# Row scaling of two RMS norms moved from VectorE to ScalarE, tile by tile

## The chip, the cores and the metric

The kernel runs on one core of a Trainium2 chip. The metric is the device time of one execution in microseconds (us), lower is better. TensorE is called PE, VectorE DVE, ScalarE ACT and GpSimd POOL, as in the profile; SP issues DMAs. Each engine runs its own instructions strictly in order, and the engines meet only at semaphores.

## The reference, cut to what matters

`x` has 64 batches of 32 rows of 128. It passes through three blocks, each added to x: a cross-attention block, two layers with delta-rule attention (x turned to 32 sequences of 64 steps), and a mixture of experts. The change is in the two layers of the middle block:

```
x = layernorm(x), turned to [32, 64, 128]
for l in range(2):
    h = x * rsqrt(mean(x * x) + 1e-6) * norm1_w[l]      # first norm ("n1")
    x = x + delta_attn(h, ...)                          # projections, chunked solve, Wo
    h = x * rsqrt(mean(x * x) + 1e-6) * norm2_w[l]      # second norm ("n2")
    g, y = split(h @ Wg[l])
    x = x + silu(g) * y @ Wd[l]
x = x * rsqrt(mean(x * x) + 1e-6) * final_norm_w
```

All data are f32. The weights norm1_w and norm2_w are applied later, after the transpose, where they lie one per partition; the norm itself multiplies each row by one number.

## The kernel before, in words

The 2048 rows of the working array R are 16 tiles of 128 rows (partitions) by 128 columns. Four tiles are a group (GT = 4, a [128, 512] piece of R), and two groups a pair: pair A is groups 0 and 1, pair B groups 2 and 3. Each pair goes through the stages of both layers and then through the experts. A string written out by hand (TURNS) says in which order the stages of the two pairs are issued, and every engine walks through the same list STEPS; within a stage it does group 0 of the pair (u = 0) and then group 1 (u = 1). So whatever an engine does for one pair stands in its queue between pieces of the other pair. There is no planner beyond that.

A norm of a group goes over four engines:

- ACT, `squares` (L869): four ACTIVATE Square over [128, 128], each with its row sum into one column of `ss[g]`; the last raises q_ss (n1) or m_ss (n2).
- POOL, `rsqrt` (L995 to L999): add eps (L998), then a power of -0.5 (L999) into `rstd[g]`; raises q_rr or m_rr.
- DVE, `rms_scaled` (L1067): one multiply of [128, 512] by rstd broadcast along the columns, into `yn[g]`; raises q_h or m_h. The stages are at L1319 (n1 of layer 1) and L1398 (n2).
- PE, `transposes` (L506): four transposes of yn into a PSUM bank; then ACT copies the bank to yT with the norm's weight (L892, L950), and the projections (n1) or the gate and up products (n2, L751 and L754) follow.

The n1 of layer 0 is another form (a layernorm and an RMS norm in one, L1308), and the final norm (`fin`, L1409) uses `rms_scaled` as well; neither is touched. yn of pair A is called yn in the profile, yn of pair B act_o. The diff touches six places in the order of STEPS: n2 of layer 0 and n1 of layer 1 for pair A, the same for pair B, then n2 of layer 1 for A and for B. What stands behind them in ACT's queue is, in this order:

- n2 of layer 0, pair A: `ah1` of pair B (evictions of the solve's second half, L926), `wt` of pair B (L933), then A's own copy to yT
- n1 of layer 1, pair A: A's own copy to yT
- n2 of layer 0, pair B: B's own copy to yT
- n1 of layer 1, pair B: B's own copy to yT, then `lout` of pair A (eight copies of the inverted blocks, L920)
- n2 of layer 1, pair A: A's own copy to yT
- n2 of layer 1, pair B: the Silu of an expert step of pair A (L979), then B's own copy to yT

Of the kernel before, what the change touches and what calls it, by code (L numbers as in the profile page):

```python
# [13 lines left out]
D = 128  # L14
NJ = 16
GT = 4
GW = GT * D
NU = 2
# [120 lines left out]
def perceiver(nc, x, ctx_t, ctx_z, ctx_last, rows, cols, w1, w2, wqkvb, wo, wgu, wd, gate_t, gate_bias,  # L139
              we_gate, we_up, we_down, sh_gate, sh_up, sh_down, ident_in, causal_in, spread_in, before_in, out):  # L140
    with ExitStack() as stack:
# [672 lines left out]
        def _(act):  # L814
# [54 lines left out]
            def squares(src, g, done):  # L869
# [3 lines left out]
                                          scale=float(D) ** -0.5, accum_out=ss[g][:, jj:jj + 1])  # L873
                last.then_inc(done, 1)

            act.wait_ge(x_done[1], NU)
            for a in range(NA):
                act.dma_start(*turned(NG - 1, a, 1)).then_inc(x_out, 16)
            act.wait_ge(masks_made, 1)
            for kind, l, pr in STEPS:  # L880
                pi = l * 2 + pr
                for u in range(NU):
# [4 lines left out]
                    if kind == "n1" and l > 0:  # L887
                        act.wait_ge(r2_ready, i - NG + 1)
                        squares(gcols(R, g), g, q_ss)
                    elif kind == "tr":  # L890
                        act.wait_ge(q_tr, i + 1)
                        copy(yT[g][:, :], b0, colv[:, C_N1 + l:C_N1 + l + 1]).then_inc(q_hT, 1)  # L892
                    elif kind in ("pj0", "pj1"):
                        part = int(kind[2])
                        act.wait_ge(q_proj, pi * 4 + part * 2 + u + 1)
                        both = psum[:, bank * 512:(bank + 2) * 512].rearrange("p (j c) -> p j c", j=2)
                        act.activation(qkv[g][:, part * 2:part * 2 + 2, :], both[:, :, 0:3 * D], ACT.Silu)
                        act.activation(th[g][:, part * 2:part * 2 + 2, :], both[:, :, 3 * D:QKVB], ACT.Tanh,
                                       scale=0.5).then_inc(q_silu, 1)
                    elif kind == "sq":  # L900
                        act.wait_ge(q_silu, pi * 4 + 2 + u + 1)
                        act.activation(sq[g].rearrange("p (j c) -> p j c", j=GT), qkv[g][:, :, 0:2 * D],
                                       ACT.Square).then_inc(q_sq, 1)
                    elif kind == "kt0":
                        act.wait_ge(k_tr, 2 * i + 1)
                        for par in range(2):
                            copy(KT[g][par], b0, head_of[par])
                        act.wait_ge(k_tr, 2 * i + 2)
                        copy(QT[g], b1).then_inc(k_bq, 1)
                    elif kind[:4] == "gram":  # L910
                        q = int(kind[4])
                        act.wait_ge(g_mm[u], pi * 4 + q + 1)
                        if q == 0:
                            act.wait_ge(q_vb, i + 1)
                        copy(quarter(GA[g], q), gram_part(bank, 0)).then_inc(g_a[u], 1)
                    elif kind == "ext":
                        act.wait_ge(g_a[u], pi * 4 + 4)
                        copy(chunks_of(pr, u),
                             GA[g].rearrange("p (n c) -> p n c", c=T)[:, :, 0:C16], chunk[0]).then_inc(s_ext0[u], 1)
                    elif kind == "lout":  # L920
                        act.wait_ge(l_inv, pi + 1)
                        lanes = back[pr].rearrange("p (n r) -> p n r", r=C16)[:, u * NB:(u + 1) * NB, :]
                        for j in range(NC):
                            last = copy(TT[g].rearrange("p (n c) -> p n c", c=T)[:, :, j * C16:(j + 1) * C16], lanes, chunk[j])
                        last.then_inc(l_out[u], 1)
                    elif kind[0] == "a":  # L926
                        half = int(kind[2])
                        act.wait_ge(s_a[u], pi * 2 + half + 1)
                        ws, us = ((b0, b1)[half].rearrange("p (t c n) -> p t c n", t=2, c=2)[:, :, c] for c in range(2))
                        copy(WU[g][:, half * 2 * D:(half + 1) * 2 * D].rearrange("p (t n) -> p t n", t=2), ws).then_inc(s_ae[u], 1)  # L930
                        copy(WU[g][:, GW:2 * GW].rearrange("p (b t n) -> p t b n", b=2, t=GT)[:, half * 2:half * 2 + 2],
                             us.rearrange("p t (b n) -> p t b n", b=2)).then_inc(s_ae[u], 1)
                    elif kind == "wt":  # L933
                        act.wait_ge(s_wt[u], pi + 1)
                        copy(WT[g], b0).then_inc(s_wte[u], 1)
                    elif kind == "onorm":
                        act.wait_ge(s_omm[u], pi + 1)
                        own = psum[:, bank * 512:(bank + 2) * 512].rearrange("p (x a e) -> p x a e", a=4, e=DK)[:, :, 0:4:3, :]
                        copy(P1[g].rearrange("p (x a e) -> p x a e", a=2, e=DK), own).then_inc(s_ocp[u], 1)
                        act.wait_ge(s_ocp[u], pi + 1)  # L940
                        act.activation(osq[g], P1[g], ACT.Square, scale=float(DK) ** -0.5).then_inc(s_osq[u], 1)
                    elif kind == "otr":
                        act.wait_ge(o_tr, i + 1)
                        copy(yT[g][:, :], b0, colv[:, C_ON + l:C_ON + l + 1]).then_inc(o_oT, 1)
                    elif kind == "n2":
                        act.wait_ge(r1_ready, i + 1)
                        squares(gcols(R, g), g, m_ss)
                    elif kind == "mtr":
                        act.wait_ge(m_tr, i + 1)
                        copy(yT[g][:, :], b0, colv[:, C_N2 + l:C_N2 + l + 1]).then_inc(m_hT, 1)  # L950
                    elif kind[:2] == "gu":
                        c = int(kind[2])
                        fn = IC[c][1]
                        act.wait_ge(m_gu, 3 * pi * NU + c * NU + u + 1)
                        if c > 0:
                            act.wait_ge(m_a, 3 * pi * NU + (c - 1) * NU + u + 1)
                        act.activation(gate[g][0:fn, :], b0[0:fn, :], ACT.Silu).then_inc(m_silu, 1)
                    elif kind == "fin":
                        act.wait_ge(r2_ready, i + 1)
                        squares(gcols(R, g), g, f_ss)  # L960
                    elif kind == "etr":
                        act.wait_ge(e_tr, g + 1)
                        copy(yT[g][:, :], b0).then_inc(e_hT, 1)
                    elif kind == "elog":
                        act.wait_ge(e_log, g + 1)
                        sg = route[pr][0]
                        act.activation(sg[:, u * GT:(u + 1) * GT, :].rearrange("p j e -> p (j e)"), b1[:, 0:GT * E],
                                       ACT.Sigmoid).then_inc(e_sig, 1)
                    elif kind == "ec":
                        act.wait_ge(e_ctr, g + 1)  # L970
                        copy(cf[g], b0[0:E, :]).then_inc(e_cf, 1)
                    elif kind in ("x0", "x1") and u == int(kind[1]):
                        p, n = l, nth(kind, l)
                        act.wait_ge(x_gate[pr], n + 1)
                        if p < 1 and n > 0:
                            act.wait_ge(x_a[pr], n)
                        elif n > 0:
                            act.wait_ge(x_gu[pr], routed(n))
                        act.activation(act_g[pr], banks[4 * pr + 2 * (n % 2)], ACT.Silu).then_inc(x_silu[pr], 1)  # L979
                    elif kind in ("end0", "end1") and u == int(kind[3]):  # L980
                        act.wait_ge(x_down[pr], (u + 1) * (NPAIR + 1))
                        copy(res[g], banks[4 * pr + 3]).then_inc(e_acc[pr], 1)
# [67 lines left out]
        def _(dve):  # L1050
# [224 lines left out]
            for kind, l, pr in STEPS:  # L1275
# [21 lines left out]
                for u in range(NU):  # L1297
# [10 lines left out]
                    elif kind == "n1" and l == 0:  # L1308
# [4 lines left out]
                        if u == NU - 1:  # L1313
                            for k in range(NU):
# [1 line left out]
                                dve.wait_ge(d_rstd, gk + 1)  # L1316
                                normed(lambda jj: gcols(X, gk)[:, jj * D:(jj + 1) * D],
                                       lambda jj: gcols(R, gk)[:, jj * D:(jj + 1) * D], gk).then_inc(q_r, 1)
                    elif kind == "n1":  # L1319
                        dve.wait_ge(q_rr, i + 1)  # L1320
                        if l == 1:
                            dve.wait_ge(q_r, g + 1)
                        rms_scaled(yn[g], gcols(R, g), g).then_inc(q_h, 1)
                    elif kind == "sq":
                        dve.wait_ge(q_silu, pi * 4 + 2 + u + 1)
                        dve.tensor_scalar(beta[g][:, :, :], th[g][:, :, :], 1.0, None, ALU.add).then_inc(q_beta, 1)
# [68 lines left out]
                    elif kind == "wo":  # L1395
                        dve.wait_ge(o_wo, i + 1)
                        dve.tensor_tensor(gcols(R, g), b1, gcols(R, g), ALU.add).then_inc(r1_ready, 1)
                    elif kind == "n2":  # L1398
                        dve.wait_ge(m_rr, i + 1)
                        rms_scaled(yn[g], gcols(R, g), g).then_inc(m_h, 1)  # L1400
                    elif kind[:2] == "gu":
                        c = int(kind[2])
                        fn = IC[c][1]
# [117 lines left out]
```

## Time and profile before

| | |
|---|---|
| three runs | 691.83, 692.78, 692.90 us; median 692.78 |
| the profiled execution | 694.24 us; its span from first to last instruction 692.4 us |
| mean granted TensorE clock | 0.878 |
| PE busy | 562.5 us (81%), weight loads 366.4 us |
| DVE busy | 442.3 us (64%), 1116 instructions |
| ACT busy | 257.3 us (37%), 576 instructions |
| POOL busy | 78.7 us (11%), 124 instructions |
| DMA | 45.67 MB, 65 GB/s over the span |

How to read it: times are of one profiled execution, counted from its first instruction. Row sums and products follow from busy times, but what an instruction costs the kernel is seen only in the chain of waits and in the timeline, where an idle time before an instruction is shown in brackets with what ended it. A line number can be that of a helper (L816 is every `copy` of ACT, L506 every transpose of a group).

### The profile page before, as it was taken

The page shows a single profiled execution, that of the slowest core. Times are in us where ns is not written, and L with a number is a line of the kernel's source. Part 1 is how long each engine was busy: PE and PEld are TensorE (multiplying, and loading weights), DVE is VectorE, ACT ScalarE, POOL GpSimd, SP SyncE. Part 2 cuts the span into 40 slices and gives each one's busy share as a digit, 9 for nine tenths or more (in the row PEclk, how much of TensorE's full clock was granted, in tenths as well). Part 3 has the DMA queues.
Part 4 walks back from the last instruction along what each step waited for, and adds up shares of the span by engine and source line. Part 5 has one row for each costly group of instructions (what it writes and reads, how often), then busy time and mean ns, then how long its engine had stood idle before and what let it go on. Part 6 is the DMA issues. An engine that isn't in the chain of part 4 may idle for free.

```text
span 692.4 us, 15649 instructions
## 1 busy us (share of the span) xinstructions
PE 562.5 (81%) x6616; PEld 366.4 (53%) x6616; DVE 442.3 (64%) x1116; ACT 257.3 (37%) x576; POOL 78.7 (11%) x124
## 2 busy tenths in 40 slices
PE   5778990767499699977688579879968899999995
PEld 2443570446499576753567558754534344444442
DVE  5785783897867535678647874794476655555553
ACT  2466530564240443552374236225223222222221
POOL 2311230630000011202120011101020000000000
PEclk9998995785556699996899879889998999999998
DMA  8788003000000000000000310003202264343331
GB/s 313 304 310 301 7 12 98 8 1 2 1 3 4 2 2 2 3 2 0 1 2 5 125 71 2 3 7 95 61 1 61 74 150 112 83 128 76 86 88 34
DMA packets 19037, 45.67 MB, mean 66 GB/s; under 512 B 3764, under 2 KB 8500, under 8 KB 18964
## 3 DMA queue, kind: packets, MB, share of 16 engines
q1 hardware_dynamic: 18648, 44.54, 20.8%
q8 instruction: 52, 0.85, 0.5%
q10 hardware_dynamic: 320, 0.13, 0.1%
q14 instruction: 17, 0.14, 0.1%
HBM read 42.30 MB, written 2.36 MB: 65 GB/s over the span
## 4 chain that ended last, share of the span: by engine, by line
PE 58%; DVE 25%; ACT 7%; issue 3%; POOL 2%; SPq 2%; DMA 2%; DVEq 0%; POOLq 0%
PE psum L793 8%; PE psum L798 7%; PE psum L788 7%; PE psum L506 4%; PE psum L635 4%; PE psum L621 3%; PE psum L751 3%; PE psum L754 3%; ACT arena L816 3%; PE psum L663 3%; PE psum L714 2%; PE psum L760 2%; DVE mid L1370 2%; DVE rowv L1368 2%; PE psum L704 2%
## 5 line engine op out<-in xcount | busy, mean ns | idle before, releaser
L979 ACT ACTIVATE arena<-psum 128x512 f32<-128x512 f32 x68 | 40.6, 597 | 126.5 <-PE psum L788 106.3
L1430 DVE TENSOR_TENSOR arena<-psum,arena 128x512 f32<-128x512 f32 x64 | 44.2, 691 | 56.8 <-PE psum L793 55.4
L798 PE MATMUL psum<-arena,wed_sb 128*128 128x512 f32 x128 | 66.2, 599 | 0.0
L621 PE MATMUL psum<-arena 32*64 32x128 f32 x1024 | 42.4, 323 | 17.8 <-DVE XA L1346 10.8
L816 ACT ACTIVATE arena<-psum 128x512 f32<-128x512 f32 (+1 forms) x72 | 34.1, 502 | 56.6 <-PE psum L621 38.5
L1435 DVE TENSOR_TENSOR arena<-arena 128x512 f32<-128x512 f32 x64 | 44.3, 693 | 14.7 <-PE psum L798 12.6
L621 PEld LDWEIGHTS psum<-arena 32*64 32x64 f32 x1024 | 36.4, 163 | 22.6 <-DVE XA L1346 11.8
L793 PE MATMUL psum<-yT,weu_sb 128*128 128x512 f32 x68 | 36.2, 614 | 11.9 <-DVE arena L1430 11.9
L506 PE MATMUL psum<-ident,yn 128*128 128x128 f32 x72 | 15.2, 367 | 36.7 <-DVE yn L1063 22.7
L798 PEld LDWEIGHTS psum<-arena,wed_sb 128*128 128x128 f32 x128 | 24.6, 192 | 31.2 <-issue 21.8
L998 POOL TENSOR_TENSOR ve<-ss,eps_rms 128x4 f32<-128x4 f32 x16 | 4.7, 291 | 292.9 <-ACT yr L872 182.5
L999 POOL TENSOR_TENSOR rstd<-ve,neg_half 128x4 f32<-128x4 f32 x32 | 35.5, 1108 | 2.5
L788 PE MATMUL psum<-yT,weg_sb 128*128 128x512 f32 x68 | 34.8, 593 | 0.0
L788 PE MATMUL psum<-w_sb,weg_sb 128*128 128x512 f32 x68 | 34.7, 592 | 0.0
L793 PE MATMUL psum<-w_sb,weu_sb 128*128 128x512 f32 x68 | 34.7, 592 | 0.0
L506 PEld LDWEIGHTS psum<-ident,yn 128*128 128x128 f32 x72 | 11.5, 190 | 40.1 <-issue 22.2
L506 PE MATMUL psum<-ident,act_o 128*128 128x128 f32 x72 | 13.6, 335 | 20.0 <-DVE act_o L1069 15.0
L793 PEld LDWEIGHTS psum<-yT,weu_sb 128*128 128x128 f32 x68 | 12.7, 193 | 29.9 <-DVE arena L1430 16.0
L816 ACT ACTIVATE yT<-psum,colv 128x512 f32<-128x512 f32 x12 | 8.0, 686 | 44.7 <-PE psum L506 44.7
L506 PEld LDWEIGHTS psum<-ident,act_o 128*128 128x128 f32 x72 | 10.1, 170 | 25.1 <-DVE act_o L1069 16.5
L760 PEld LDWEIGHTS psum<-wd_sb,arena 128*128 128x128 f32 (+1 forms) x192 | 21.9, 191 | 2.2 <-DVE arena L1405 2.2
L635 PE MATMUL psum<-mid,arena 64*64 64x32 f32 x512 | 18.6, 237 | 5.4 <-ACT arena L816 5.4
(294 smaller groups left out, 1172.7 us busy)
## 6 DMA issues: line engine op xcount, KB each, us to landing
arena<-shares SPq DMA_DIRECT2D x64, 256.0 KB, 4.0
arena<-in_ctx_t SPq DMA_DIRECT2D x16, 514.0 KB, 8.3
arena<-in_ctx_z SPq DMA_DIRECT2D x16, 512.0 KB, 9.6
XA<-in_x SPq DMA_DIRECT2D x2, 512.0 KB, 4.9
weg_sb<-in_we_gate SPq DMA_DIRECT2D x2, 512.0 KB, 6.1
weu_sb<-in_we_up SPq DMA_DIRECT2D x2, 512.0 KB, 7.0
wed_sb<-in_we_down SPq DMA_DIRECT2D x2, 512.0 KB, 7.6
x_mid<-XA SPq DMA_DIRECT2D x28, 32.0 KB, 1.9
```

The lines of the kernel that those rows point to most:

```text
L506: last = pe.transpose(bank[:, jj * D:(jj + 1) * D], src[u][:, jj, :], ident[:, :])
L621: last = pe.matmul(banks[bank + hh][s2 * T:(s2 + 1) * T, m * D:(m + 1) * D].rearrange("p (c q) -> p c q", c=2), KT[g][par][rows_, c0:c0 + ...
L635: last = pe.matmul(two_parts(bank[rows_, :], t % 2, h), lhs[rows_, n * T:(n + 1) * T], two_parts(rhs[rows_, :], t, h), start=True, stop=True)
L760: last = pe.matmul(b0[:, jj * D:(jj + 1) * D], hm[g][0:fn, c, jj * D:(jj + 1) * D], wd_sb[0:fn, l, c, :], start=(c == 0), stop=(c == 2))
L788: pe.matmul(banks[4 * pr + 2 * (n % 2)], weg_sb[:, w, :], yT[g][:, :], start=True, stop=True).then_inc(x_gate[pr], 1)
L793: pe.matmul(x1, weu_sb[:, w, :], yT[g][:, :], start=True, stop=True).then_inc(x_up[pr], 1)
L798: pe.matmul(x3, wed_sb[:, (p - 1) % (NPAIR + 1), :], act_a[pr], start=(p == 0), stop=False, skip_group_check=True).then_inc(x_down[pr], 1)
L816: return act.activation(out_, in_, ACT.Copy, scale=scale)
L979: act.activation(act_g[pr], banks[4 * pr + 2 * (n % 2)], ACT.Silu).then_inc(x_silu[pr], 1)
L999: pool.tensor_tensor(rstd[u][:, 0:n], v, neg_half[:, 0:n], ALU.pow).then_inc(done, 1)
L1430: dve.tensor_tensor(act_gu[pr], banks[4 * pr + 1], act_g[pr], ALU.mult).then_inc(x_gu[pr], 1)
L1435: dve.tensor_tensor(act_a[pr], share[pr][k % 2][:, (p % PER) * GW:(p % PER + 1) * GW], act_gu[pr], ALU.mult).then_inc(x_a[pr], 1)
```

## The change

For the touched norms the multiply is taken off DVE. ACT gets a helper `by_row` that waits for rstd of a group and scales its four tiles one by one, each by an ACTIVATE Copy over [128, 128] whose scale is a column of rstd. It is issued for both groups of a pair, behind the squares of the second group. Semaphore values stay as they were; DVE's wait for q_r at n1 goes with its step.

```diff
+            def by_row(g, i, ready, done):
+
+                act.wait_ge(ready, i + 1)
+                for jj in range(GT):
+                    last = copy(yn[g][:, jj, :], gcols(R, g)[:, jj * D:(jj + 1) * D], rstd[g][:, jj:jj + 1])
+                last.then_inc(done, 1)
+
...
                     if kind == "n1" and l > 0:
                         act.wait_ge(r2_ready, i - NG + 1)
                         squares(gcols(R, g), g, q_ss)
+                        if u == NU - 1:
+                            for k in range(NU):
+                                by_row(pr * NU + k, l * NG + pr * NU + k, q_rr, q_h)
...
                     elif kind == "n2":
                         act.wait_ge(r1_ready, i + 1)
                         squares(gcols(R, g), g, m_ss)
+                        if u == NU - 1:
+                            for k in range(NU):
+                                by_row(pr * NU + k, l * NG + pr * NU + k, m_rr, m_h)
...
-                    elif kind == "n1":
-                        dve.wait_ge(q_rr, i + 1)
-                        if l == 1:
-                            dve.wait_ge(q_r, g + 1)
-                        rms_scaled(yn[g], gcols(R, g), g).then_inc(q_h, 1)
...
-                    elif kind == "n2":
-                        dve.wait_ge(m_rr, i + 1)
-                        rms_scaled(yn[g], gcols(R, g), g).then_inc(m_h, 1)
```

## Rows read from the trace of the kernel before

**Rows 1.** The chain that ended last, by engine (share of the span)
```profile
PE 58%; DVE 25%; ACT 7%; issue 3%; POOL 2%; SPq 2%; DMA 2%; DVEq 0%; POOLq 0%
```
**Rows 2.** Instructions of line L1069: duration ns min/median/max, first and last start
```profile
L1069 DVE TENSOR_TENSOR yn<-R,rstd x8: 679/691/693, 248.8 to 431.2; 128x512 f32<-128x512 f32 x8
```
**Rows 3.** Groups of ACT by form: busy us, mean ns, idle before
```profile
L816 ACT ACTIVATE arena<-yr,small 128x512 f32<-128x512 f32 x16 | 10.0, 708 | 3.3 <-DVE yr L1375 3.3
L872 ACT ACTIVATE yr<-R 128x128 f32<-128x128 f32 x32 | 9.4, 296 | 8.0 <-DVE R L1408 4.2 <-DVE R L1397 3.8
L846 ACT ACTIVATE yn<-yr,shift,rstd 128x128 f32<-128x128 f32 x16 | 6.4, 481 | 0.0
```
**Rows 4.** Timeline of ACT: start us, length us, instructions merged
```profile
26.41 3.17 ACT L846 ACTIVATE yn<-yr,shift,rstd 128x128 f32<-128x128 f32 x8
345.10 4.99 ACT L816 ACTIVATE arena<-yr,small 128x512 f32<-128x512 f32 x8
```
**Rows 5.** Chain in order of time, 246 to 252 us: start, length
```profile
246.28 3.85 PE psum L635 x128
250.14 1.14 PE psum L689 x8
```
**Rows 6.** Timeline around n2 of layer 0, pair A
```profile
247.79 1.01 POOL L999 TENSOR_TENSOR rstd<-ve,neg_half 128x4 f32<-128x4 f32 x1
248.51 0.63 ACT L816 ACTIVATE arena<-psum 128x256 f32<-128x256 f32 x2
248.83 0.69 DVE L1069 TENSOR_TENSOR yn<-R,rstd 128x512 f32<-128x512 f32 x1 [1.81 <-POOL rstd L999]
249.04 1.34 POOL L999 TENSOR_TENSOR rstd<-ve,neg_half 128x4 f32<-128x4 f32 x1
250.18 0.66 ACT L816 ACTIVATE arena<-psum 128x256 f32<-128x256 f32 x2 [1.05 <-PE psum L635]
```
**Rows 7.** Timeline around n1 of layer 1, pair A
```profile
272.78 1.01 POOL L999 TENSOR_TENSOR rstd<-ve,neg_half 128x4 f32<-128x4 f32 x1
275.37 1.27 ACT L816 ACTIVATE yT<-psum,colv 128x512 f32<-128x512 f32 x2 [2.94 <-PE psum L506]
```
**Rows 8.** Timeline around n2 of layer 0, pair B
```profile
314.37 1.52 POOL L999 TENSOR_TENSOR rstd<-ve,neg_half 128x4 f32<-128x4 f32 x1
316.40 1.97 PE L506 MATMUL psum<-ident,act_o 128*128 128x128 f32 x8 [7.98 <-DVE act_o L1069]
317.55 0.69 ACT L816 ACTIVATE w_sb<-psum,colv 128x512 f32<-128x512 f32 x1 [4.91 <-PE psum L506]
```
**Rows 9.** Timeline around n1 of layer 1, pair B
```profile
339.10 1.03 POOL L999 TENSOR_TENSOR rstd<-ve,neg_half 128x4 f32<-128x4 f32 x1
340.04 1.89 DVE L1375 STREAM_TRANSPOSE yr<-mid 128x1024 f32<-128x1024 f32 x1
341.80 1.25 DVE L1069 TENSOR_TENSOR act_o<-R,rstd 128x512 f32<-128x512 f32 x2
344.52 0.69 ACT L816 ACTIVATE w_sb<-psum,colv 128x512 f32<-128x512 f32 x1 [0.17 <-PE psum L506]
```
**Rows 10.** Timeline around n2 of layer 1, pair A
```profile
406.33 1.13 POOL L999 TENSOR_TENSOR rstd<-ve,neg_half 128x4 f32<-128x4 f32 x1
407.79 1.97 PE L506 MATMUL psum<-ident,yn 128*128 128x128 f32 x8 [3.88 <-DVE yn L1069]
```
**Rows 11.** Timeline around n2 of layer 1, pair B
```profile
477.75 0.57 ACT L979 ACTIVATE arena<-psum 128x512 f32<-128x512 f32 x1
478.81 1.34 POOL L999 TENSOR_TENSOR rstd<-ve,neg_half 128x4 f32<-128x4 f32 x1
480.19 0.69 DVE L1069 TENSOR_TENSOR act_o<-R,rstd 128x512 f32<-128x512 f32 x1 [0.90 <-POOL rstd L999]
481.43 1.02 PE L751 MATMUL psum<-w_sb,wgu_sb 128*128 128x512 f32 x2
```
**Rows 12.** Windows: busy us and instructions of each engine, PEclk, DMA share, GB/s
```profile
338.00:340.00 2.00, 0.00 (x0) 0.00 (x0) 1.74 (x10) 0.67 (x5) 1.65 (x3) 0.83 0.00 0
```

## The prediction, made before the changed kernel was run

> **What bounds the kernel now.** I read the chain of waits first. PE is 58% of it, DVE 25% and ACT only 7% [rows 1], so neither the DVE time removed nor the ACT time added can be booked by its length: what counts is which of the two ends last in each of the six places that the change touches. The instructions of L1069 come next [rows 2]: a scaling is one DVE instruction of 0.69 us. There are 16, four belong to the final norm and stay, so 12 go, 8.3 us of DVE. Then I read ACT's groups by form and ACT's timeline for what a tile will cost there [rows 3, 4], and last the timeline of each place, in the order of the kernel, asking of each what stands behind the scaling in the queues of DVE and ACT.
>
> **What one group costs on ACT.** The trace has no [128, 128] ACTIVATE from SBUF with a scale per partition and nothing else. The nearest rows lie on both sides: Square with a fixed scale takes 296 ns, Identity with a scale and a bias per partition 481 ns [rows 3]. One such operand should lie in the middle, 388 ns. What counts in a sequence is the distance from start to start. For the Identity that is (3.17 - 0.48) / 7 = 0.384 us, for the 512-wide Copy with one such scale (4.99 - 0.71) / 7 = 0.612 us [rows 3, 4]; both are 0.097 below the length. So 0.388 - 0.097 = 0.29 us from tile to tile: ACT is held for 1.17 us by a group, and the last tile is done 1.26 us after the first started. I take this. The upper bound is 0.384 (1.54 us a group, done after 1.63); the lower one is the Square without any such operand, 0.296 - 0.097 = 0.20. A group thus takes 1.26 us where DVE takes 0.69, and 12 groups put 14 us on ACT. The wait of ACT for POOL is new as well: `by_row` stands in ACT's queue, and all behind it waits until both groups have their rstd and are scaled.
>
> The Trainium skill speaks against the change here: ScalarE: Activation LUTs, Rules for kernel authors, says to put a multiply on VectorE and not on ScalarE. By length alone the trace agrees, 0.69 against 1.26 us; what it would give here is a rival below.
>
> **Place 1, n2 of layer 0, pair A: +1.55 us.** ACT's squares end at 248.5 and it goes straight to the evictions of `ah1` of pair B (248.51 and 250.18); PE ends L635 and starts the transposes of `wt` (L689) at 250.14 at once, which need those evictions and end at 251.28 [rows 5, 6]. This is on the chain. After: rstd of group 0 is there at 248.80, so the first four tiles hold ACT from 248.85 to 250.03. The second power on POOL took 1.34 us beside the DVE multiply against 1.01 us for the first [rows 6]; with that multiply gone I take 1.01, so rstd of group 1 comes at 250.05 and ACT is free at 251.26. The first eviction is done 0.38 later at 251.64, PE starts at 251.7 in place of 250.14, and the second group's gate puts its end at 252.8 in place of 251.28. Behind it PE is busy without a gap to 270, so all of it is kept: +1.55 (1.4 to 2.4 with the upper price). The DVE is idle there and gives nothing back.
>
> The Trainium skill, SBUF — State Buffer, Who interferes with whom, has a reason for this: a DVE instruction with two SBUF inputs shuts a reading GpSimd instruction out for its whole length. The row of 1.34 agrees in sign (0.33 more); taken literally it would put this second power's start at 249.52 and its end at 250.53 before, against 250.38 measured. Without the effect places 1 and 6 would each lose 0.33 more.
>
> **Place 2, n1 of layer 1, pair A: 0.** DVE scaled both groups at 273.91, after the second rstd (272.78 + 1.01 = 273.79) [rows 7]. ACT, idle since its squares, scales group 0 from 272.4, group 1 from 273.84, done at 275.1. PE is busy with pair B until 274.75 anyway and takes group 0's transposes then; the copy to yT starts at 275.37 [rows 7] as before. With the upper price ACT is free at 275.4: +0.1.
>
> **Place 3, n2 of layer 0, pair B: -0.1.** DVE is late here: it scaled at 315.66 behind the solve's extraction, and both PE (idle for 8 us) and ACT waited for it [rows 8]. ACT can scale group 0 from 313.7 (the first power ended 0.7 before the second began) and group 1 from 315.95 (rstd at 314.37 + 1.52 = 315.89), free at 317.1. PE transposes group 0 at 315.05, but group 1 only at 317.25, and the gate product that follows stands behind these in PE's queue: 318.25, where before PE had L506 done at 316.40 + 1.97 = 318.37. DVE's own chain starts 1.28 sooner, but its next product needs PE. Between -0.5 and +0.4.
>
> **Place 4, n1 of layer 1, pair B: -1.9 us.** The same, but stronger. rstd of group 1 is ready at 339.10 + 1.03 = 340.13; DVE is in the 1.89 us transpose of the solve and scales only from 341.80 to 343.05, PE follows, and ACT's second copy to yT ends at 345.21. Then `lout`, 4.99 us of ACT, begins [rows 4, 9]; it needs only that transpose (done at 341.93) and sits in ACT's queue behind the copies, on the chain. After: group 0 scaled by 339.9, group 1 from 340.2 to 341.45, the transposes of group 1 on PE from 341.5, 1.15 us later (as from 316.40 to 317.55 [rows 8]) the second copy at 342.65, done at 343.34. `lout` starts 1.9 us sooner. Bounds: -1.5 with the upper price, -2.4 if PE's clock has not fallen by then.
>
> **Place 5, n2 of layer 1, pair A: +0.1.** rstd of group 1 at 406.33 + 1.13 = 407.46; DVE scaled at 407.04 to 408.33 and PE ended the eight transposes at 407.79 + 1.97 = 409.76 [rows 10]. ACT: group 1 from 407.5 to 408.75, its transposes on PE from 408.8 to 409.8. Equal within 0.1; I add a little for a clock that may rise later. -0.4 to +0.6. DVE is freed 1.3 us for the solve of pair B, whose result ACT fetches only behind A's last gate product.
>
> **Place 6, n2 of layer 1, pair B: +0.9 us.** Behind the squares ACT had the Silu of an expert step (477.75), then the copy of group 0 at 480.04; PE's gate product started at 481.43 [rows 11]. After: group 0 from 478.63, rstd of group 1 at 478.81 + 1.01 = 479.82, scaled from 479.9, ACT free at 481.08; then the Silu (0.57) and the copy (0.69), so the product starts at 482.4. PE is busy behind it until 505, so +0.9 to +1.0 is kept; +1.5 with the upper price.
>
> **Sum:** 1.55 + 0 - 0.1 - 1.9 + 0.1 + 0.9 = +0.55 us. The profiled execution would go from 694.24 to 694.8; it lies 1.46 us over the median of the runs shown, so the same step on the median gives 692.78 + 0.55 = 693.3 us. No DMA is issued or moved by the change.
>
> **Rivals.**
> - *ACT is held as long as by the Identity.* If a tile costs 0.384 us, the six places give 2.35 + 0.1 + 0 - 1.5 + 0.2 + 1.5 = +2.65: 695.4 us, slower. For it speaks that this is the only 128-wide row with a per-partition operand; against it that its price falls with each operand it has. It decides from about 0.33 us a tile.
> - *PE's clock drops in place 1.* This ends slower too. PE gets a new idle time of 1.6 us at 250.1. In place 4, in an idle time of 5.9 us, the granted clock goes to 0.83 in the window 338 to 340 [rows 12], that is from 2.4 to 1.2 GHz some 3 us into it. If it fell at 252, in a stretch where PE has no gaps, 4 us of PE work would take twice the time: about +2, 695.3 us. Against it: the gap is half as long.
> - *The freed DVE time counts.* If DVE's solve is what bounds places 3 and 5, the 1.28 us freed in each move the chain: 0.55 - 1.2 - 1.2 = -1.9, 690.9 us, faster. For it: DVE is the releaser of PE in both. Against it: by my timelines DVE's next product waits for PE or ACT each time.
> - *Every group pays its extra length.* If queues gave nothing back, 12 groups would lose 1.26 - 0.69 = 0.57 us each, +6.8: 699.6 us. The rule on ScalarE above, from the Trainium skill, would have it so. Against it: in places 2, 3 and 5 the extra length lies beside PE's or POOL's work.
>
> **How the numbers follow.** The sum as worked out has 0.53, the dearer tile 0.15, the clock 0.12, the DVE relief 0.17, the full extra length 0.03. About 0.2% (1.4 us) is what a measurement of this kernel can tell from no change. The forecast holds mostly inside it, with 0.04 of its chance each side; so faster is 0.13 of the relief's and 0.04, 0.17; slower is 0.15 + 0.12 + 0.03 + 0.04 = 0.34; same is the rest, 0.49. The bounds of the six places added run from -1.0 to +3.5, which is 691.8 to 696.3 us; all six at their worst together is unlikely, so I end at 695.6, and reach down to 691.0 to take in half of the relief's chance.
>
> **What would show it.** L1069 remains with 4 instructions; a new group of 48 ACTIVATE into yn and act_o with 0.39 us each and 0.29 from start to start; the second L999 in places 1 and 6 at 1.01; PE's L689 starting 1.5 us later relative to the end of L635; `lout` starting about 1.9 us earlier relative to the last L1408 of pair B in layer 0; PEclk still 1.00 from 250 to 270. The prediction is wrong if a tile is held longer than 0.33 us, if PE's clock falls in place 1, or if DVE's pieces of the solve turn out to be what PE waits for behind places 3 and 5.

## The result, and the profile after

| | before | after |
|---|---|---|
| median of the paired runs | 692.84 us (8 runs) | 697.71 us (8 runs, 693.2 to 702.1) |
| ratio, 95% interval | | 1.0075 [1.0049, 1.0100] |
| profiled span | 692.4 us | 697.4 us |
| mean granted clock, profiled | 0.878 | 0.871 |

Forecast were 693.3 us and a range of 691.0 to 695.6: the measured time lies above it, and the whole interval of the ratio lies above 1. All ratios here leave out executions more than 1.5% over the fastest of their own kernel: seven in all, three of them of the version with all places but place 1.

What the change does by itself is as foreseen. ACT's groups by form (busy us, mean ns, idle before): 48 ACTIVATE of 388 and 389 ns, in the middle of the two rows that bounded it [rows 3].

```profile
L816 ACT ACTIVATE act_o<-R,rstd 128x128 f32<-128x128 f32 x24 | 7.6, 389 | 3.1 <-POOL rstd L1012 3.1
L816 ACT ACTIVATE yn<-R,rstd 128x128 f32<-128x128 f32 x24 | 7.6, 388 | 0.8 <-POOL rstd L1012 0.8
```

**Place 1**, timeline, beside [rows 6]:

```profile
247.36 1.01 POOL L1012 TENSOR_TENSOR rstd<-ve,neg_half 128x4 f32<-128x4 f32 x1
248.40 2.53 ACT L816 ACTIVATE yn<-R,rstd 128x128 f32<-128x128 f32 x8 [0.23 <-POOL rstd L1012]
248.62 1.01 POOL L1012 TENSOR_TENSOR rstd<-ve,neg_half 128x4 f32<-128x4 f32 x1
250.84 1.18 ACT L816 ACTIVATE arena<-psum 128x256 f32<-128x256 f32 x4
251.26 1.97 PE L689 MATMUL psum<-ident,arena 128*128 128x128 f32 x8 [1.55 <-ACT arena L816]
```

Eight scalings hold ACT for 2.44 us, the evictions follow at 250.84, PE stands idle for 1.55 us; the second power takes 1.01 us and no longer 1.34. All that was in the sum. What was not is the length of PE's work behind: eight transposes take 1.97 us here and 1.14 in [rows 5]. The windows of 2 us say why (columns as in [rows 12]):

```profile
250.00:252.00 2.00, 0.74 (x4) 0.75 (x5) 0.00 (x0) 2.00 (x8) 0.00 (x0) 0.73 0.00 0
252.00:254.00 2.00, 2.00 (x11) 2.00 (x10) 0.00 (x0) 1.22 (x3) 0.00 (x0) 0.50 0.00 0
```

The granted clock goes to 0.50 (1.2 GHz) at 250.9, 0.3 us before the idle time ends, and back to 2.4 GHz at 254.3, with PE busy throughout the second window. In the three other traces with a fall here (a second one of the changed kernel, place 1 alone, six places with fillers elsewhere) it comes between 0.2 us before and 0.4 us after PE starts again. In the kernel before the same stretch was at 1.00:

```profile
250.00:252.00 2.00, 2.00 (x22) 1.73 (x18) 0.69 (x1) 1.82 (x5) 0.39 (x1) 1.00 0.00 0
```

**Place 4**, timeline of the changed kernel, beside [rows 9]:

```profile
341.48 1.28 ACT L816 ACTIVATE act_o<-R,rstd 128x128 f32<-128x128 f32 x4 [0.33 <-POOL rstd L1012]
342.81 0.89 PE L506 MATMUL psum<-ident,act_o 128*128 128x128 f32 x4 [0.95 <-ACT act_o L816]
344.33 4.99 ACT L816 ACTIVATE arena<-yr,small 128x512 f32<-128x512 f32 x8
350.13 4.47 PE L663 MATMUL psum<-wqkvb_sb,w_sb 128*128 128x392 f32 x8 [2.32 <-ACT th L908]
```

The window behind its end:

```profile
350.00:352.00 2.00, 1.87 (x3) 1.17 (x4) 0.00 (x0) 0.85 (x4) 0.00 (x0) 0.50 0.00 0
```

`lout` starts at 344.33, 7.27 us after the squares (337.06), in place of 9.36 (345.10 [rows 4], squares at 335.74), a gain of 2.1. But the second half of the projections, which waits for it, takes 4.47 us, with the clock at half from 349.9 to 353.3, where the chain of before had it at 2.92, and most of the gain is gone.

**Place 6**, timeline, beside [rows 11]:

```profile
482.45 2.53 ACT L816 ACTIVATE act_o<-R,rstd 128x128 f32<-128x128 f32 x8 [0.76 <-POOL rstd L1012]
484.89 0.58 ACT L992 ACTIVATE arena<-psum 128x512 f32<-128x512 f32 x1
485.04 0.66 PE L506 MATMUL psum<-ident,act_o 128*128 128x128 f32 x4 [0.60 <-ACT act_o L816]
486.09 1.75 PE L751 MATMUL psum<-w_sb,wgu_sb 128*128 128x512 f32 x2 [0.40 <-ACT w_sb L816]
```

Its window with the fall:

```profile
486.00:488.00 2.00, 1.91 (x3) 0.96 (x4) 0.88 (x2) 0.61 (x2) 0.00 (x0) 0.61 0.02 4
```

PE has no idle time over 0.8 us here (0.76, 0.60 and 0.40), and the clock falls all the same, at 486.4 for 3.4 us.

**The ledger by stretch.** So that a place can be read apart from what came before it, I measure from the start of its first Square (L872) to the first instruction of a line of PE, in each trace, a weight load counted like a matmul. Two traces of the unchanged kernel before agree in these within 0.02 us, but for place 5 to L760 (0.08). All in us:

```
                                       forecast   before   changed  difference
place 1  squares to L689                 +1.55      3.91      5.53     +1.62
         squares to L751 (gate product)             7.02     10.00     +2.98
place 2  squares to projections           0         7.64      7.64      0.00
place 3  squares to L751                 -0.1       8.08      7.73     -0.35
place 4  squares to 2nd half of L663     -1.9      15.16     13.08     -2.08
         squares to the solve's products           17.99     17.48     -0.51
place 5  squares to L751                 +0.1       6.64      6.49     -0.15
         squares to L760 (down product)            17.54     19.35     +1.81
place 6  squares to L751                 +0.9       5.91      6.83     +0.92
         squares to L760                           23.90     26.51     +2.61
```

The first line of each place is the queue's share. They add to 1.62 + 0 - 0.35 - 2.08 - 0.15 + 0.92 = -0.04 us, against +0.55 forecast. In some places the first weight load runs ahead of its matmul (by 0.21 us at L751 in places 3 and 5 of the changed kernel, by 0.11 in place 6 of before); by the first matmul the differences there are -0.14, +0.07 and +0.81, and the sum is +0.28. By either count it is a few tenths.

The second lines add what is lost behind: 1.36 us in place 1, 1.57 in 4, 1.96 in 5, 1.69 in 6, and 2.02 more between the final norm of pair A and place 6: 8.6 us. In place 4 the half clock is as long as before but lies over PE's work now; in the other stretches it is longer than before. The stretches that are left (up to place 1, behind places 3 and 4, behind place 6) came out 3.6 us shorter; the half clock around place 3, for one, lasts 10.2 us in place of 13.7. -0.04 + 8.6 - 3.6 = 5.0, the difference of the spans.

Not all of this belongs to the place where it appears. The losses of places 1, 4 and 6 (4.6 us) appear only in traces where that place has moved. The loss of place 5 does not: in three versions below where DVE scales there as before (p1_half, p34_only, p6_only) place 5 to L760 is 18.74, 19.12 and 19.09 us, and in one where ACT does (all_fill1) it is 17.77. It and the 2.02 us are nearly made up by the 3.6 us gained elsewhere.

### The profile page after: what moved, and what is told of

It reads as the page before. It is cut to its first block, busy times and chain, and to the rows that moved or that the text cites. A ratio compares the mean times of both kernels' runs of the same rounds, so it can differ in the third digit from the quotient of the medians.

```text
span 697.4 us, 15680 instructions
## 1 busy us (share of the span) xinstructions
PE 571.4 (82%) x6616; PEld 370.4 (53%) x6616; DVE 434.6 (62%) x1104; ACT 272.1 (39%) x624; POOL 78.1 (11%) x124
## 4 chain that ended last, share of the span: by engine, by line
PE 57%; DVE 23%; ACT 10%; POOL 4%; issue 3%; SPq 2%; DMA 1%; DVEq 0%; POOLq 0%
PE psum L793 8%; PE psum L788 8%; PE psum L798 7%; PE psum L751 3%; PE psum L506 3%; PE psum L621 3%; PE psum L754 3%; PE psum L635 3%; PE psum L663 3%; ACT arena L816 3%; PE psum L760 2%; PE psum L714 2%; POOL rstd L1012 2%; SPq L450 2%; PE psum L704 2%
## 5 line engine op out<-in xcount | busy, mean ns | idle before, releaser
L788 PE MATMUL psum<-yT,weg_sb 128*128 128x512 f32 x68 | 36.6, 621 | 0.0
L1388 DVE TENSOR_TENSOR arena<-psum,small 128x512 f32<-128x512 f32 x24 | 15.9, 687 | 18.2 <-PE psum L704 18.0
L760 PEld LDWEIGHTS psum<-wd_sb,arena 128*128 128x128 f32 (+1 forms) x192 | 21.9, 191 | 2.2 <-DVE arena L1410 2.2
```

Source lines behind the costliest of these rows:

```text
L760: last = pe.matmul(b0[:, jj * D:(jj + 1) * D], hm[g][0:fn, c, jj * D:(jj + 1) * D], wd_sb[0:fn, l, c, :], start=(c == 0), stop=(c == 2))
L788: pe.matmul(banks[4 * pr + 2 * (n % 2)], weg_sb[:, w, :], yT[g][:, :], start=True, stop=True).then_inc(x_gate[pr], 1)
```

## The experiments

Every ratio is to the kernel before on the same chip, with its 95% interval. The forecasts set two theories against each other: A, queues as priced plus half-clock stretches that PE's new or shifted idle times bring; B, queues priced too low. A set ON_ACT chooses the places; the others keep DVE's multiply.

```diff
-                    elif kind == "n2":
+                    elif kind == "n2" and (kind, l, pr) not in ON_ACT:
...
+                        if u == NU - 1 and (kind, l, pr) in ON_ACT:
+                            for k in range(NU):
+                                by_row(pr * NU + k, l * NG + pr * NU + k, m_rr, m_h)
```

### Place 1 alone, and all but place 1

> Only place 1 (n2 of layer 0, pair A) is scaled by ACT; the other five stay on DVE. Both theories expect L689 to start 1.5 to 1.6 us later, against the start of L872 of that norm, than in the kernel before (1.59 in the changed kernel). Theory A (queue and clock: the new idle time of PE costs clock as well): a stretch of half clock of about 3.4 us appears behind it, near 251 us, and PE is 2.4 to 2.8 us late at the first L751 behind it; the time is 2 to 4 us over before (+0.3 to +0.6%), because the clock pattern behind can change once more. Theory B (the queue alone; the half-clock stretches are a matter of chance from run to run): no half-clock stretch there, PE 1.6 us late at L751, time +1.6 us (+0.2%).

> All places but place 1 are scaled by ACT. The changed kernel is 0.75% slower than before. Theory A: the 2.4 to 2.8 us of place 1 are gone, the clock losses of places 4, 5 and 6 may remain; +0.2 to +0.5% over before. Theory B (queues priced too low everywhere): about 1.6 us less than the changed kernel, +0.5%. If place 1 alone starts the whole pattern of half-clock stretches, it comes to before or under it, 0 to -0.2%.

Place 1 alone: 1.0058 [1.0039, 1.0076]. Squares to L689 5.52 us, to L751 10.06, half clock for 3.4 us at 251.8: theory A's numbers; B's +1.6 us to L751 is excluded by its +3.0. The time is at the top of what A allowed. All but place 1: 1.0037 [1.0011, 1.0064]. This is inside A's range, but B's +0.5% lies in the interval as well, and the median of all twelve executions is 696.99 us against 692.27 (+0.7%): the time of this run decides nothing between them. Its trace has the losses of places 4, 5 and 6 (squares to L760 19.42 and 26.50 in the last two). So place 1 doesn't start the pattern of the others. The two ratios add to 0.95%, which the intervals allow for the whole (0.75%).

### Places 3 and 4 alone

> Only places 3 and 4 (n2 of layer 0 and n1 of layer 1, pair B), where DVE was late, are scaled by ACT. Both theories: `lout` and the Silu behind it start 1.9 to 2.0 us earlier than before. Theory A: PE's idle time ahead of the second half of the projections grows to over 3.2 us, the clock falls there as in the changed kernel (half clock near 350 to 353 us), which takes back 1.3 us, so PE is only 0.6 us early behind it; the time is -0.5 to -2 us, within 0.3% of before. Theory B: full clock, 1.9 us early and kept: -0.3%.

1.0027 [1.0001, 1.0053]. Squares to the second half of L663 13.07 (15.16 before), to the solve's products 17.47: the 2.1 us are there and 1.6 go again, as A had it. But A's reason was wrong: PE's idle time ahead of the second half did not grow, it shrank from 2.75 to 2.31 us, and the clock fell nonetheless. The time, +1.9 us, is above A's -0.5 to -2 us.

### Fillers in place 1

```diff
                     elif kind == "wt":
+                        if l == 0 and pr == 1 and u == 0:
+                            pe.wait_ge(s_ae[u], pi * 4 + 2)
+                            dense(b0, 4)
                         pe.wait_ge(s_ae[u], pi * 4 + 3)
```

> The changed kernel's six places, and four more bf16 matmuls of [96, 512] whose result nobody reads (0.38 us each at full clock) in PE's queue ahead of the late transposes (L689) of place 1, so that PE isn't idle there; no data depend on them. Theory A: the half-clock stretch at 251 to 254 us is gone, PE is 1.6 us late at L751 in place of 2.4 to 2.8, the time 1 us or more below the changed kernel (under +0.6%). Theory B: the clock isn't tied to the idle time, nothing changes (+0.75%) or it gets slower by what the fillers overrun (0.1 us).

Its windows over the same stretch:

```profile
250.00:252.00 2.00, 1.43 (x10) 0.72 (x8) 0.00 (x0) 2.00 (x9) 0.00 (x0) 1.00 0.00 0
252.00:254.00 2.00, 2.00 (x60) 1.83 (x62) 0.00 (x0) 2.00 (x5) 0.00 (x0) 1.00 0.00 0
```

The clock stays at 1.00; squares to L689 is 5.52 as without the fillers, to L751 8.61 in place of 10.00. That is the split of place 1: 1.6 us by the queue, 1.4 by the clock. The time doesn't show it: 1.0086 [1.0057, 1.0115] from six executions, not below the changed kernel; there A missed. Place 6, which has no filler in this version, lost its fall too: squares to L760 is 24.80 and not 26.51.

### ACT held without its result being used, and half of the hold

In the first, DVE scales as before and ACT does the same eight scalings into a dead buffer; in the second, group 0 goes to ACT and group 1 stays on DVE:

```diff
+                                act.wait_ge(m_rr, k + 1)
+                                for jj in range(GT):
+                                    copy(gate[k][:, jj * D:(jj + 1) * D], gcols(R, k)[:, jj * D:(jj + 1) * D],
+                                         rstd[k][:, jj:jj + 1])
```
```diff
-                            for k in range(NU):
-                                by_row(pr * NU + k, l * NG + pr * NU + k, m_rr, m_h)
+                            by_row(0, 0, m_rr, m_h)
```

> All scaling stays on DVE; in place 1 ACT does the same waits and the same eight scaling instructions as in the changed kernel, into a buffer that nobody reads, so ACT is held but yn comes from DVE as before. Theory A (the hold of ACT's queue is what place 1 costs, and the clock follows): from the start of the squares to L689 5.5 to 5.9 us (3.91 before, 5.53 in the changed kernel; up to 0.3 more, since DVE's multiply slows POOL again), to the first gate product 10.0 to 10.4 (7.02, 10.00), a half-clock stretch of 3.4 us at 251. Theory B (it is the slower scaling itself, four tiles where one instruction stood): both stay near 3.9 and 7.0, as the scaled rows come when they came before.

> In place 1 only group 0 is scaled by ACT, group 1 stays on DVE, so ACT is held until 250.0 in place of 251.3. Theory A: PE's new idle time shrinks from 1.55 to about 0.35 us; from the squares to L689 4.2 to 4.4 us, and the clock doesn't fall, so the first gate product comes 7.3 to 7.5 us after the squares (7.02 before, 10.00 changed): half of ACT's hold gives a sixth of the loss. Theory B (loss in proportion to the ACT work): half of both, 4.7 and 8.5.

Timeline of the first:

```profile
250.18 1.34 POOL L1016 TENSOR_TENSOR rstd<-ve,neg_half 128x4 f32<-128x4 f32 x1
251.56 0.69 DVE L1086 TENSOR_TENSOR yn<-R,rstd 128x512 f32<-128x512 f32 x1 [0.90 <-POOL rstd L1016]
253.16 1.19 PE L690 MATMUL psum<-ident,arena 128*128 128x128 f32 x8 [1.89 <-ACT arena L817]
```

Squares to the late transposes 5.87 us: it is the hold of ACT's queue, not the scaling's length, that place 1 pays, and with DVE's multiply back the second power takes 1.34 us again. But squares to the gate product is 8.95 and not the 10.0 to 10.4 of theory A: the clock did not fall, after a longer idle time (1.89 us) than in the changed kernel (1.55):

```profile
252.00:254.00 2.00, 0.84 (x7) 0.73 (x8) 0.25 (x1) 2.00 (x8) 0.00 (x0) 1.00 0.00 0
```

So the length of an idle time does not decide alone. Time: 1.0052 [1.0017, 1.0088]. The half hold: 4.27 us to the transposes, 7.36 to the gate product, clock at 1.00, as A forecast and not in proportion; 1.0027 [1.0003, 1.0052].

### Place 6 alone

> Only place 6 (n2 of layer 1, pair B) on ACT. Theory A: from the squares to the gate product 6.83 us (5.91 before), and a half-clock stretch of 3.4 us behind it, if the clock falls there by itself and not because of what came before: 26.5 us from the squares to the first L760 of the down product (23.90 before). Theory B (the fall there is left over from the earlier places): 6.83 and 24.8.

Squares to L751 6.83, but to L760 24.81: theory B's number for the second, and the window behind is at full clock. Theory A missed here.

```profile
484.00:486.00 2.00, 2.00 (x6) 0.84 (x5) 0.54 (x1) 0.60 (x1) 0.00 (x0) 1.00 0.00 0
```

With the same idle times (0.76, 0.60, 0.40) the clock fell in the changed kernel and not here. 1.0001 [0.9979, 1.0022].

### Fillers wherever PE waits long, in both versions

`dense(bank, n)` issues n bf16 matmuls that nobody reads.

```diff
+FILL_MTR = {(0, 1): 16, (1, 0): 8}
...
+                        if u == 0 and (l, pr) in FILL_MTR:
+                            dense(b0, FILL_MTR[l, pr])
...
-                            dense(b0, 6)
+                            dense(b0, 22 if (l, pr) == (1, 0) else 6)
```

> The kernel before, with bf16 matmuls of [96, 512] whose result nobody reads in PE's queue where PE waits for over 2.5 us on other engines in both versions: 16 and 8 ahead of the transposes of places 3 and 5, 8 at place 4, 6 between the two halves of the projections there, 16 more ahead of the output transposes of layer 1, pair A, 10 ahead of the transposes of the routing of pair A. It is the reference for the next run. Theory A (the clock follows PE's idle times): the half-clock stretches between 308 and 411 us and that at 459 go or shrink, and the time falls by 3 to 7 us (-0.4 to -1.0%). Theory B: PE's work there isn't what the chain waits for; within 0.2%.

> The six places on ACT, with the same fillers as base_fill. Theory A (queue and clock): with the clock held, what is left of the change is what the queues cost, +0.5 us by the sum of the prediction and up to +2 with the clock drop of place 1, which has no filler; so 0 to +0.3% over base_fill, against +0.75% without fillers. Theory B (the queues were priced too low): the full +0.7% over base_fill remains.

> Places 3 and 4 on ACT, with the same fillers. Theory A: the 1.9 us of place 4 are kept now, 1.5 to 2.5 us below base_fill (-0.2 to -0.35%), the fastest of all. Theory B: as without fillers, 0 to +0.3% over base_fill.

> all_fill with fillers in places 1 (4 matmuls) and 6 (2, 1 and 1) as well. Theory A: 8.4 to 8.7 us from the squares to the gate product in place 1 (10.12 without), 24.8 from the squares to the down product in place 6 (26.51 without), so 3 us less than all_fill in those two places; the time within 0.2% of base_fill. Theory B: the same time as all_fill.

```
                                          ratio [95%]             place 1   place 4    place 6
                                                                  to L751   to solve   to L760
fillers, all norms on DVE                 1.0005 [0.9978, 1.0032]   7.02     17.81      23.90
fillers, six places on ACT                1.0016 [0.9986, 1.0045]  10.12     15.67      26.51
the same, fillers in places 1 and 6 too   1.0008 [0.9979, 1.0037]   8.62     15.67      24.81
fillers, places 3 and 4 on ACT            1.0038 [1.0009, 1.0068]   7.01     15.91      23.79
```

With PE busy in those waits in both versions, the change costs 0.11% and, with places 1 and 6 filled, 0.03%, in place of 0.75%; theory B wanted +0.7%. Each interval is 0.3% either way, so the difference of two of them is known to about 0.4%: +0.7% is out, a smaller cost is not. The mean granted clock of the timed runs says the same: 0.887 and 0.886 in the first two versions, where without fillers it was 0.877 for the kernel before and 0.866 for the changed one.

The local distances support it, most of all in place 4: its 2.1 us are kept in all four traces where both place 4 is on ACT and fillers stand (15.67 to 15.91 to the solve), and mostly lost in all six with the move and no filler near place 4 (17.47 to 17.83, where before has 17.99). In place 1 the fall is gone in both traces with a filler there and present in four of the five without. In place 6 the filler proves little: the fall is absent with it (24.81), but also without it in p6_only and all_fill1.

Two things A missed: the fillers do not make the kernel before faster (0.4 to 1.0% was expected), though its clock is higher, so half clock in PE's long waits costs it nothing that these times can show. And the version with places 3 and 4 came out slower, not fastest. Its trace has half clock from 376 to 400, where the other versions with fillers ran at full clock to 394 or later.

### The same programs once more

> The kernel before, unchanged, for a second trace. Both theories: the same time within 0.2%. Theory A: its half-clock stretches differ from those of the first trace where code is the same (as p1_only's did at 220 us), and the instructions of those stretches are late by up to 5 us and catch up again where PE isn't what the chain waits for. Theory B: the same stretches.

> The changed kernel, unchanged, for a second trace and more times. Theory A (queue terms that repeat, clock losses that vary with where PE's idle time falls): the queue terms repeat within 0.05 us (squares to L689 5.53, squares to the gate product in place 6 6.83, to the second half of the projections in place 4 13.08); if the half-clock stretches differ, the losses behind them do too, with 1.4 us at place 1 and 1.7 at place 6 each there or not; over all, times 0.4 to 0.9% over before and spread wider than before's. Theory B (the 5 us are in the queues): all local times and all half-clock stretches as in the first trace.

Before: 1.0014 [0.9988, 1.0039], and against A's expectation its trace has the same half-clock stretches as the first. Changed: 1.0068 [1.0044, 1.0091], so the slowdown stands. Its queue terms repeat (5.53, 7.74, 6.50 and 6.83; 13.29 in place 4, where 13.08 was measured first), and so do the losses behind them (10.18, 17.63, 19.35, 26.51), though the pattern ahead of place 1 is another one (half clock from 171 to 246 without a break). Over all timed runs the mean granted clock is 0.877 in 122 runs of the kernel before and 0.866 in 20 of the changed one. From run to run the two go together in some kernels only: the correlation of a run's time with its time at half clock is 0.81 in the 12 runs of this last and 0.38 in the 8 of the first result, but 0.02 over the 122 runs of the kernel before, so the total of half clock does not give the time by itself; where it falls would have to matter, which the timed runs cannot show.

### Candidates

> The candidate: places 3, 4 and 5 on ACT, where DVE was late, with the fillers of base_fill. Theory A: from base_fill the queues give 0.3 + 1.9 + 1.0 us, so -3 us or -0.4% against base_fill, and about as much against the kernel before, if chance half-clock stretches elsewhere let it be seen; in the trace 15.7 to 15.9 us from the squares to the solve in place 4 and 16.3 to the down product in place 5. Theory B: no gain against base_fill.

> Places 3, 4 and 5 on ACT, without fillers. Theory A: the queues give 0.35 + 2.1 + 0.15 us; the clock takes back 1.6 in place 4 and up to 1.8 in place 5; -0.3 to +0.3% against before, in the middle the 0 that p34_only points to. Theory B: -2.6 us, -0.37%.

1.0009 [0.9974, 1.0043] with fillers, 1.0018 [0.9994, 1.0041] without. In the first, place 4 to the solve is 15.67 and place 5 to L760 16.63, as wanted, but half clock between the final norm and place 6 takes it back; in the second place 5 is 18.69. No version here beats the kernel before.

## Why the prediction was wrong

- **ACT's price** (0.29 us a tile, 1.26 a group, from rows on either side): right, 388 ns and 2.44 us for two groups. The rival with 0.384 us is out.
- **Places 1, 4 and 6**: right in mechanism and size, +1.62, -2.08 and +0.92 against +1.55, -1.9 and +0.9. p1_hold shows that the first is the queue's hold.
- **Places 2, 3 and 5**: right within 0.25 us. POOL's second power shorter by 0.33: right, 1.01 us in places 1 and 6.
- **"Behind it PE is busy without a gap to 270, so all of it is kept: +1.55"**: this is the step that failed. The 1.6 us of delay came as forecast. What is lost besides is PE's work behind it at half clock, 1.4 us more. The prediction had this as a rival for place 1 alone, with a chance of 0.12, at about +2 us (its working, 4 us of work taking twice the time, would give +4; measured were 3.4 us at half clock and 1.4 us lost); it happened there, in four of the five traces where both groups hold ACT and no filler stands in the gap.
- **"`lout` starts 1.9 us sooner" in place 4 and "+0.9 to +1.0 is kept" in place 6**: the starts were right, and the same step, that the work behind keeps its length, failed twice more (1.57 us in place 4, where all six traces with the move and no filler near it show a fall, and 1.69 us in place 6, where four of the six with the move and no filler there do). Place 5 lost 1.96 us too, but its own move does not explain that (see the ledger).
- **What the clock needs to fall**: the prediction asked only whether PE's idle time came near the one of place 4 before (5.9 us, [rows 12]). Half clock came with idle times of 1.55 us, of 2.3 us, and of three pieces of 0.4 to 0.8 us. The trace of the kernel before already had such a case, in rows that the prediction did not use: with idle times of 0.83 and 0.59 us and four transposes between them, the clock is at half from 438.3, in the second of them, to 441.7 (two timeline rows, and the window over the fall).

```profile
437.18 0.66 PE L506 MATMUL psum<-ident,yn 128*128 128x128 f32 x4 [0.83 <-DVE yn L1063]
438.43 1.12 PE L506 MATMUL psum<-ident,yn 128*128 128x128 f32 x4 [0.59 <-DVE yn L1063]
438.00:440.00 2.00, 1.57 (x24) 1.24 (x28) 1.57 (x4) 0.89 (x2) 0.00 (x0) 0.58 0.00 0
```

- **The freed DVE time counts**: out. Place 3 gained 0.35 us and not 1.2. The squares of place 4 do come 1.26 us sooner behind it, but they do so in p1_only and p1_half too (1.06 and 1.29), where place 3 is unchanged and the half clock there is as short; in no_p1, with place 3 moved and the half clock as long as before, it is 0.25.
- **The rule of the Trainium skill** (ScalarE: Activation LUTs, Rules for kernel authors: a multiply goes on VectorE), which stood beside the rival that every group pays its extra length: the full extra length, 6.8 us, isn't what the queues cost; they cost next to nothing in sum. That the sign of the result agrees with the rule is by another cause.

What stays open: why the clock fell in one build and not in another at the same place and the same idle times (p6_only, p1_hold). The traces show that the half-clock stretches begin at other moments relative to the kernel's work from build to build; whether that decides it is not shown, as no run varied it alone. Also open is how the timed runs divide over the places. Place 1 alone costs more in them (0.58%, 4.0 us) than its 3.0 us in the trace, places 3 and 4 cost 0.27% where their trace gains 0.5 us locally, and removing the fall in place 1 (all_fill1) did not lower the time. One trace is one execution: the mean granted clock of the timed runs of the kernel before goes from 0.862 to 0.888, where both its traces have 0.878, so many timed runs have other half-clock stretches than the traces show. That the local losses of the traces are what slows the timed runs is therefore supported by the fillers and by the mean clocks, and not shown place by place.

## What to carry to other kernels

When a change moves waits about, price TensorE's work behind each new idle time also at half clock, here even for idle times of 1.55 us or of three pieces of 0.4 to 0.8 us, and look through the whole trace of before for the shortest idle time with a fall of the granted clock ahead of the sum. An instruction moved to an engine with spare time costs what stands behind it in that queue until its input is there; that sum can be made from the timeline to a few tenths of a us per place. It was right here, and it was not the result.

## What the runs showed that was not expected

- TensorE fell to 1.2 GHz for 3.4 us in an idle time of 1.55 us (changed kernel, place 1), and did not in or behind one of 1.89 us (p1_hold).
- With a filler of four bf16 matmuls in the gap of 1.55 us it stayed at 2.4 GHz (in both traces with that filler), and 1.4 us came back locally.
- With fillers in the long waits of the kernel before, the mean granted clock of its timed runs rose from 0.877 to 0.887 and its time did not fall (1.0005).
- In seven of the seventeen traces a stretch of identical code (about 220 to 230 us) ran at half clock where it ran at full clock before: in p1_only the matmuls of L725 were 5.1 us late there, and PE caught all of it up by 233 us, since it was not what the chain waited for.
